# Spreading table gathers over attention blocks, splitting the value products, and reordering the last block of a recommendation tower

## The reference

```
h   = gelu(layernorm(x @ W1.T + b1))                # two branches, real and imaginary
s   = (h @ W2.T + b2).reshape(B, 4, 512)            # four states of 512 each
q, k, v = s @ Wq.T, s @ Wk.T, s @ Wv.T              # real and imaginary, 8 heads of 64
w   = softmax(|q conj(k)| / 8) over the 4 states
attn = (w @ v) @ Wo.T                               # output projection
R, I = attn through int_W[n] of each state          # "vectors", complex
f   = cos(phase difference of states i, j) * strength[i, j]
sup = sum_j f * (R, I)[j];  normalise;  measure;  post layer;  three top layers
strength[b, f, :] = tbl_f[ids[b, f]]                # four lookup tables, rows of 4 floats
```

## Time and profile before

| | |
|---|---|
| median of 3 runs | 3205.1 us (3201.33 to 3205.56) |
| the profiled execution | 3230.8 us, span 3229.1 us |
| PE busy | 3002.5 us, 93% of the span |
| DVE busy | 1566.5 us, 49% |
| ACT busy | 1118.1 us, 35% |
| POOL busy | 311.4 us, 10% |
| granted TensorE clock, mean | 0.972 of 2.4 GHz |

### The profile page before, as it was taken

How to read it: one execution, slowest core, us unless ns; L and a number is a source line. 1 busy time by engine, 2 the same in 40 slices (tenths; PEclk the granted TensorE clock), 3 DMA queues, 4 the chain that set the end, 5 groups by cost and what they waited for, 6 DMA issues and landing times. The chain is left out here.

```text
span 3229.1 us, 43945 instructions
## 1 busy us (share of the span) xinstructions
PE 3002.5 (93%) x15808; PEld 2578.3 (80%) x15808; DVE 1566.5 (49%) x2779; ACT 1118.1 (35%) x1889; POOL 311.4 (10%) x289
## 2 busy tenths in 40 slices
PE   7999999999699999999759999999999989898798
PEld 6888888888588877888658999999999977676686
DVE  3222222221621216111156766767667658888873
ACT  3111111110421115111135555545545555454454
POOL 1000000000111101011130000000000003324200
PEclk9999999999899999999979999999999999999899
DMA  5222222221533325233332232231231374444410
GB/s 193 75 71 75 75 71 75 73 64 38 179 118 101 97 66 169 76 97 101 109 101 66 53 91 65 65 91 52 77 79 52 98 176 90 93 91 84 117 62 11
DMA packets 364352, 285.48 MB, mean 88 GB/s; under 512 B 280192, under 2 KB 280320, under 8 KB 364160
## 3 DMA queue, kind: packets, MB, share of 16 engines
q1 hardware_dynamic: 341632, 206.97, 24.0%
q0 software_dynamic: 22656, 77.67, 6.9%
HBM read 194.40 MB, written 90.18 MB: 88 GB/s over the span
## 5 line engine op out<-in xcount | busy, mean ns | idle before, releaser
L50 PE MATMUL banks<-a_whi,a_xhi 128*128 128x512 f32 x1152 | 450.1, 391 | 24.2 <-DVE a_wlo L179 17.7
L52 PE MATMUL banks<-a_whi,a_xlo 128*128 128x512 f32 x1152 | 449.0, 390 | 0.0
L51 PE MATMUL banks<-a_wlo,a_xhi 128*128 128x512 f32 x1152 | 448.9, 390 | 0.0
L50 PE MATMUL banks<-b_ghi,b_whi 128*128 128x512 f32 x1024 | 401.9, 392 | 10.0 <-DVE b_slo L389 8.8
L52 PE MATMUL banks<-b_ghi,b_wlo 128*128 128x512 f32 x1024 | 398.9, 390 | 0.0
L51 PE MATMUL banks<-b_glo,b_whi 128*128 128x512 f32 x1024 | 398.8, 389 | 0.0
L179 DVE TENSOR_TENSOR a_wlo<-a_wraw,a_whi 128x512 fp32r<-128x512 f32 x144 | 99.6, 691 | 577.3 <-ACT a_whi L165 577.3
L50 PE MATMUL banks<-t_sx,s_whi 128*128 128x256 f32 x1024 | 293.3, 286 | 58.4 <-DVE s_wlo L1309 24.1
L165 ACT ACTIVATE a_whi<-a_wraw 128x512 fp32r<-128x512 f32 x144 | 91.3, 634 | 667.2 <-PE banks L52 628.4
L374 DVE TENSOR_TENSOR b_wlo<-b_wraw,b_whi 128x512 fp32r<-128x512 f32 x128 | 88.2, 690 | 445.0 <-ACT b_whi L326 444.8
L52 PE MATMUL banks<-t_sx,s_wlo 128*128 128x256 f32 x1024 | 290.0, 283 | 0.0
(11 more groups left out here) (159 smaller groups left out, 5641.2 us busy)
## 6 DMA issues: line engine op xcount, KB each, us to landing
a_wraw<-w_first SPq DMA_DIRECT2D x144, 256.0 KB, 2.6
b_wraw<-w_second SPq DMA_DIRECT2D x128, 256.0 KB, 2.6
t_sx<-s_scr SPq DMA_DIRECT2D x64, 512.0 KB, 4.6
a_scr<-t_at SPq DMA_DIRECT2D x256, 128.0 KB, 2.1
s_axng<-a_scr SPq DMA_DIRECT2D x64, 512.0 KB, 6.0
s_wraw<-w_pieces SPq DMA_DIRECT2D x82, 256.0 KB, 4.6
h_scr<-a_hst POOLq DMA_DIRECT2D x72, 256.0 KB, 2.7
b_hl<-h_scr POOLq DMA_DIRECT2D x16, 1024.0 KB, 5.9
```

Source lines behind the costliest of these rows:

```text
L50: mm(out, ahi, bhi, start=first, stop=False)
L51: mm(out, ahi, blo, start=False, stop=False)
L52: return mm(out, alo, bhi, start=False, stop=last)
```

## The change

- POOL: before each tile t of four gathers, a wait for `projected >= (t + 2) * 8 + 5`, so that tile t is gathered in block t + 2, after the query product of its slice 2. The 32 gathers fall in blocks 2 to 9.
- PE, in blocks 1 to 14: `values(b, 3)` moves from ahead of the four `project_out` to between the second and the third.
- ACT, in blocks 1 to 14: `v_evac(b, 3)` moves behind `t_magnitude`, `exponent` and the first two `t_high`.
- The tail of block 15: `t_turn`, `pt_evac` and `spread` of slices 1 to 3 come ahead of `mix`, `o_high` and `o_low` of the slice before.
- SP: `load(0, 2)` moves ahead of the last 8 weight pieces and of the wait for the last output projection.

```
# SP
+            load(0, 2)
             sp.wait_ge(wo_full, LAST_B * 4 + 4)
             for i in range(NP + 6 * KD, 2 * NP):
                 piece(i)
-            load(0, 2)
# POOL
             for t in range(TT):
+                pool.wait_ge(projected, (t + 2) * 8 + 5)
# ACT, block
-                for i in range(4):
+                for i in range(3):
                     v_evac(b, i)
+                if first or last(b):
+                    v_evac(b, 3)
                 t_magnitude(b)
                 exponent(b)
                 if not first and not last(b):
-                    for m in range(KD):
-                        t_high(b - 1, m)
+                    t_high(b - 1, 0)
+                    t_high(b - 1, 1)
+                    v_evac(b, 3)
+                    t_high(b - 1, 2)
+                    t_high(b - 1, 3)
# ACT, tail
             t_high(LAST_B - 1, 2)
+            pt_evac(LAST_B, 1)
             o_high(LAST_B, 0)
-            pt_evac(LAST_B, 1)
             pieces(NP + 2, NP + 4)
             t_high(LAST_B - 1, 3)
+            pt_evac(LAST_B, 2)
             o_high(LAST_B, 1)
-            pt_evac(LAST_B, 2)
+            pt_evac(LAST_B, 3)
             o_high(LAST_B, 2)
-            pt_evac(LAST_B, 3)
# DVE, tail
             t_low(LAST_B - 1, 2)
+            spread(LAST_B, 2)
             o_low(LAST_B, 0)
-            spread(LAST_B, 2)
             pieces(NP + 2, NP + 4)
             t_low(LAST_B - 1, 3)
+            spread(LAST_B, 3)
             o_low(LAST_B, 1)
-            spread(LAST_B, 3)
# PE, block
                 values(b, 2)
+                if not first and not last(b):
+                    project_out(b - 1, 0)
+                    project_out(b - 1, 1)
                 values(b, 3)
                 if not first and not last(b):
-                    for m in range(KD):
-                        project_out(b - 1, m)
+                    project_out(b - 1, 2)
+                    project_out(b - 1, 3)
# PE, tail
             project_out(LAST_B - 1, 2)
+            t_turn(LAST_B, 1)
             mix(LAST_B, 0)
-            t_turn(LAST_B, 1)
             project_out(LAST_B - 1, 3)
+            t_turn(LAST_B, 2)
             mix(LAST_B, 1)
-            t_turn(LAST_B, 2)
+            t_turn(LAST_B, 3)
             mix(LAST_B, 2)
-            t_turn(LAST_B, 3)
             mix(LAST_B, 3)
```

## The result

Six runs of each: 3218.6 us (3216.1 to 3221.6) against 3203.9 us (3200.2 to 3205.6), ratio 1.0051, 95% interval 1.0041 to 1.0061. The forecast was 3183 us, faster. The profiled execution of the changed kernel took 3217.2 us, as much as its timed runs, with a span of 3215.5 us: 13.6 us shorter than that of the kernel before, while the timed runs are 14.7 us longer.

The account below looks back on a forecast made before the run. PE was taken to bound attention, so only its idle time counted. The terms -31.4 + 14.0 - 2.7 - 1.9 = -22.0 us took the median from 3205.1 to 3183.1 us, with a range of 3171 to 3207.

Parts of the forecast that it names:

- The gathers: Between blocks 0 and 1: without late signals PE restarts at 1668.4, not 1699.8; 31.4 us less.
- rival C: Gap at block 1: late signals are smaller without a profiler, so less is won; 3191 to 3209 us; chance 0.20.
- The split: Blocks 1 to 14: 0.3 us for `o_low` plus 0.7 us behind the stores in each; 14.0 us more.
- `load(0, 2)`: Load of state 2, vectors stage: issued at 2627.1 instead of 2633.02, there before PE wants it; 2.7 us less.
- The tail: After block 15's softmax: reordered DVE and ACT work lets `o_low(3)` end at 2601.9, against 2605.76; 1.9 us less.
- the profile gains 30 us and the median does not: Sign that the prediction is wrong, comparing the profiled execution with the median of timed runs.
- 31.4 and not 33.6: PE's restart in block 1: a shorter gap might keep the high clock, making the gathers' term 33.6; 31.4 was kept.

Follow-up runs that it names:

- e2: Kernel before with only the gathers spread over blocks 2 to 9: 3199.1 us against 3225.1, ratio 0.9914 (0.9900 to 0.9928).
- e6: Kernel before without its 32 gathers, POOL setting a constant instead: 3200.4 us against 3201.7, ratio 0.9996.
- e1: Kernel before, unchanged, for a second profile: 3228.4 us in its one run; the kernel before took 3225.1 us on this chip.
- e8: Kernel before with the split value products, and SP storing result slices 0 and 1 ahead of the second half of the states: 3213.6 us, ratio 1.0033.
- e3: Kernel before with only the fourth value product moved between the output projections (PE and ACT, blocks 1 to 14): 3246.9 us, ratio 1.0062.
- e14: Kernel before with spread gathers and split, the first output projection waiting for its last slice nine matmuls later: 3203.6 us, ratio 1.0010.
- e5: The changed kernel, all parts, against the kernel before in a later job: 3216.8 us against 3201.7, ratio 1.0045.
- e9: The changed kernel again, against the kernel before in another job: ratio 1.0055 (1.0042 to 1.0069).
- e12: The changed kernel again, against the kernel before in another job: ratio 1.0046 (1.0030 to 1.0063).
- e15: The changed kernel again, against the kernel before in another job: ratio 1.0051 (1.0035 to 1.0066).
- e7: Kernel before with all 32 gathers in one run from slice 2 of block 5: 3199.7 us, ratio 0.9993; repeats 1.0001, 0.9999 and 1.0002.

## Why the prediction was wrong, step by step

*The gathers, -31.4 us: the step that failed for the timed runs.* In the profiled executions it was right: SP's first issue in block 1 moved from 1738.39 to 1707.30, 31.1 us, and e2 measured 25.9 us (23 to 32 by its interval) in timed runs on one chip. But the prediction then subtracted it from the median, 3205.1 us, of runs that did not hold the gap. The profiled execution of before was 25.7 us above that median, and rival C was there for it, with the right reading that the gap need not be in the timed runs. It was shut out in size: it was granted 25.7 us at most, which left 5.7 us to win and an upper end of 3209. e6 shows that in timed runs without the gap leaving the gathers out wins nothing clear of noise (4 us at most). With 0 in their place, and the other terms as forecast, the sum would have been 3205.1 + 14.0 - 2.7 - 1.9 = 3214.5. What set the timed runs apart was not the profiler, as C put it. On the chip of e1 before is long with and without it, at a mean granted clock of 0.971 to 0.973 (0.976 or 0.977 in e2); on four other chips no timed run of before is over 3205.4 us, and the profile of e8, on one of them, has the gathers in place and no gap. The profile of before took 3230.8 us, like the chip of e1, and the first timed runs 3200.2 to 3205.6, like the four others. That they came from two chips is the likely reading; the record doesn't say.

*The split, +14.0 us: right in mechanism, 3.9 us too small.* All three steps came as worked out: PE waits for `o_low`, 1.32 us beyond the modelled end of a matmul (1.2 forecast); `q_evac` is late behind the stores, 0.78 us (0.7 forecast); a block takes 60.22 us (60.0 forecast). From the first issue in block 1 (31.1 us earlier than before) to the first weights after the blocks (2555.74 before, 2542.55 after, 13.2 us earlier) the blocks cost 17.9 us. e3, e8 and e14 each show one of the waits by what they do to it.

*`load(0, 2)`, -2.7 us: the negation took more back.* State 2, which PE began at 2641.38 behind an idle 2.92 us, now begins at 2624.64 with no wait for its load. But later in that state PE waits for ACT's negation, which stands behind the eight weight pieces that now come after the load:

```profile
2629.20 0.50 PE L50 MATMUL banks<-s_whi,s_axng 128*128 128x512 f32 x1 [1.61 <-ACT s_axng L1025]
```

```profile
2622.68 5.43 ACT L983 ACTIVATE s_whi<-s_wraw 128x512 fp32r<-128x512 f32 x8 [6.41 <-DMA s_wraw<-w_pieces]
2628.02 1.13 ACT L1025 ACTIVATE s_axng<-s_axng 128x512 fp32r<-128x512 f32 x2
```

The wait that went was worth 3.1 us from matmul to matmul, the one that came takes 1.8: 1.3 us less.

*The tail, -1.9 us: it gave 0.5 us.* The vectors stage starts at 2602.22, 13.7 us before the old 2615.89, and the blocks had ended 13.2 us earlier. I had overlooked that `o_high(15, 0)` waits for all output projections of block 14, whose operand it overwrites. ACT stands idle for that, `o_low(0)` on DVE stands behind it, and the third `spread` and the turn of PE behind that:

```profile
2574.08 1.93 ACT L949 ACTIVATE t_ohi<-banks,cols 64x256 fp32r<-64x256 f32 x4 [1.85 <-PE banks L52]
```

```profile
2576.04 1.99 DVE L1295 SCALAR_TENSOR_TENSOR t_olo<-banks,cols,t_ohi 64x256 fp32r<-64x256 f32 x4 [2.03 <-ACT t_ohi L949]
...
2580.43 1.13 DVE L1286 SCALAR_TENSOR_TENSOR t_pd<-t_ex,t_inv,mask 128x128 f32<-128x128 f32 x4
```

```profile
2581.62 1.12 PE L1658 MATMUL banks<-ident,t_pd 128*128 128x128 f32 x4 [6.00 <-DVE t_pd L1286]
```

Together 17.9 - 1.3 - 0.5 = 16.1 us more from the rows of the two profiles, against 14.7 to 17.0 us in the five comparisons of timed runs (the first, e5, e9, e12, e15). With the 31.1 us of the gap that makes 15.0 us less, while the span got 13.6 us shorter; where the other 1.4 us went was not followed. The prediction had named what would make it wrong, among it that the profile gains 30 us and the median does not. It was that one, at the gap itself: 31.1 us there in the profile, none in the median.

PE restarted at 1668.60, 1668.4 by the prediction, behind 3.92 us of idle time. The clock was no better for the shorter gap: in the 5 us from there PE ran 23 matmuls at a granted clock of 0.50, as the 23 at 0.51 of the earlier trace rows. Keeping 31.4 and not 33.6 for the gathers was right.

```profile
1668.60:1673.60 5.00, 5.00 (x23) 5.00 (x24) 0.25 (x1) 1.88 (x4) 0.00 (x0) 0.50 0.00 0
```

**What stays open.** What in a run of gathers holds up PE on one chip, and why it does not on the others. Late signals are one reading. But PE itself also stands without any wait that the profile shows, for 10.8 us in before and through the nine matmuls in 15 us of e1, so PE's own program may be what is held up; no run tells the two apart. e2 changed both the place of the gathers and the length of their run, so it does not show which of the two counts: e7 and its repeats, made for that, never met that chip. What the whole changed kernel takes there was not measured either. The ratios of e2 and e3 multiply to 0.9976, so with the tail and the load one would put it at some 8 to 10 us under before: an estimate, and no more certain than those two intervals.

## What to carry to other kernels

If the profiled execution is longer than the timed runs and one odd gap is about as large as the difference, the gap may be in no timed run: cost its removal at nothing there as one whole case, not at what is left of it by subtraction. A product moved forward to cover a wait uncovers what it covered before: look for the wait of the instruction that now comes earlier, and, on the engine that issues transfers, for what is queued behind the signal that now comes later. Where the wait stems from work that another engine does too late, reorder that engine: one copy moved on ScalarE gave 1.27 us a block, where moving PE's product took 1.2.

## What the runs showed that I had not expected

The same kernel takes 3223 to 3233 us on one chip and 3198 to 3206 us on four others. On the one, spreading 32 gathers of 128 rows each, issued back to back, took 25.9 us off; on the others no run shows a gap, with the same run of gathers at the old place (e8) or in block 5 (e7 and its repeats). In the gap PE's signals seem to arrive up to 31.7 us late, or PE itself is slowed to one matmul in 2.1 or 2.8 us, while the DMA engines are busy for a share of 0.04 to 0.07 (a stretch of e1, columns as in rows 1):

```profile
1682.50:1697.50 15.00, 2.46 (x9) 1.66 (x7) 0.00 (x0) 0.00 (x0) 8.35 (x9) 0.61 0.04 1
```

Four gathers at a time, one group in each block, leave no mark on that chip (e2: blocks of 58.93 us).
